# Twelve rows of inverse sums turned and spread by DMA in a two-layer graph attention kernel, with new slots

## The reference, cut to what matters

```
h = relu(layernorm(x))                       # before each layer
# layer 0: q, k, v = h W + b; scores = q k^T / sqrt(32) + beta * adj, masked where adj <= 0
x = x + softmax(scores) @ v
# layer 1: q, k, v from h; a = q k^T / sqrt(384) + adj
pad_mask = all(a == 0, over the keys)        # such rows give zeros
o = nan_to_num(softmax(where(pad_mask, -inf, a))) @ v
x = x + o @ Wo.T + bo
```

## Time and profile before

| what | value |
|---|---|
| median of 3 runs | 2241.57 us |
| the profiled execution's own time | 2242.91 us |
| its span (first to last instruction) | 2241.1 us |
| PE busy | 2165.6 us, 97% |
| ACT busy | 2044.9 us, 91% |
| DVE busy | 1825.2 us, 81% |
| POOL busy | 1529.3 us, 68% |
| DMA queue of SP, share of 16 DMA engines | 69.1% |

### The profile page before, as it was taken

How to read it: one execution, slowest core, us unless ns; L and a number is a source line. 1 busy time by engine, 2 the same in 40 slices (tenths; PEclk the granted TensorE clock), 3 DMA queues, 4 the chain that set the end, 5 groups by cost and what they waited for, 6 DMA issues and landing times.

```text
span 2241.1 us, 75523 instructions
## 1 busy us (share of the span) xinstructions
PE 2165.6 (97%) x19968; PEld 1424.7 (64%) x19968; DVE 1825.2 (81%) x10186; ACT 2044.9 (91%) x7816; POOL 1529.3 (68%) x2439
## 2 busy tenths in 40 slices
PE   3889999999999999999999999999999999999997
PEld 1556666666666666666666666666666666666665
DVE  4678888888888888888888888888888888888777
ACT  3879999999999999998999999999999999999987
POOL 4458667676677676676776676776676776676565
PEclk9999999999999999999999999999999999999999
DMA  8667676886676776676776766976666887867651
GB/s 188 136 129 138 124 140 135 136 158 123 138 144 134 136 157 123 138 140 123 152 133 134 144 134 134 153 132 136 144 132 134 155 128 137 146 131 129 132 107 45
DMA packets 461311, 303.36 MB, mean 135 GB/s; under 512 B 228432, under 2 KB 460880, under 8 KB 460880
## 3 DMA queue, kind: packets, MB, share of 16 engines
q1 hardware_dynamic: 460880, 298.45, 69.1%
HBM read 71.83 MB, written 25.17 MB: 43 GB/s over the span
## 4 chain that ended last, share of the span: by engine, by line
PE 83%; DVE 6%; issue 4%; ACT 3%; POOL 1%; SPq 1%; DMA 1%; DVEq 0%; ACTq 0%; POOLq 0%
PE job_bank L886 45%; PE pt_bank L909 13%; PE o_bank L922 8%; PE score_bank L899 7%; PE inv_bank L945 3%; PE post_bank L959 2%; PE post_bank L955 2%; PE post_bank L956 2%; ACT probs L583 2%; PE post_bank L937 2%; DVE neg L691 1%; DVE part_lo L757 1%; DVE inv_wide L749 1%; DVE off_zero L740 1%; DVE live L744 1%
## 5 line engine op out<-in xcount | busy, mean ns | idle before, releaser
L583 ACT ACTIVATE probs<-neg,neg_max 128x128 f32<-128x128 f32 x3072 | 1189.6, 394 | 60.8 <-DVE neg_max L691 60.7
L886 PE MATMUL job_bank<-h,w_hi 128*128 128x512 f16 x2304 | 725.0, 381 | 41.1 <-DMA h<-h_rows 37.1
L583 ACT ACTIVATION_READ_ACCUMULATOR probs<-neg,neg_max 128x1 f32 x3072 | 595.1, 194 | 0.0
L608 ACT ACTIVATE probs_t<-pt_bank 128x512 f32<-128x512 f32 x768 | 449.8, 586 | 32.9 <-PE pt_bank L909 30.1
L909 PE MATMUL pt_bank<-ident,probs 128*128 128x128 f32 x3072 | 465.0, 274 | 10.7 <-ACT probs_t L608 9.9
L886 PE MATMUL job_bank<-h,w_lo 128*128 128x512 f16 x1152 | 438.2, 380 | 0.0
L909 PEld LDWEIGHTS pt_bank<-ident,probs 128*128 128x128 f32 x3072 | 366.7, 141 | 93.9 <-issue 13.7
L886 PE MATMUL job_bank<-w_hi,h 128*128 128x384 f16 x1536 | 414.3, 327 | 7.7 <-DVE v L771 7.5
L520 POOL TENSOR_TENSOR pair_sum<-neg 128x256 f32<-128x256 f32 x384 | 281.2, 732 | 190.4 <-DVE neg_max L691 176.1
L691 DVE CUSTOM_DVE_ANT_0 neg<-score_bank,bias 128x128 f32<-128x128 f32 x1536 | 353.9, 286 | 24.1 <-issue 22.4
L886 PEld LDWEIGHTS job_bank<-h,w_hi 128*128 128x128 f16 x2304 | 221.9, 98 | 232.7 <-issue 49.9
(11 more groups left out here) (57 smaller groups left out, 3547.0 us busy)
## 6 DMA issues: line engine op xcount, KB each, us to landing
stack<-part_hi SPq DMA_DIRECT2D x768, 128.0 KB, 3.4
stack<-part_lo SPq DMA_DIRECT2D x384, 128.0 KB, 3.6
x_norm<-in_x SPq DMA_DIRECT2D x32, 768.0 KB, 6.1
x_res<-in_x SPq DMA_DIRECT2D x32, 768.0 KB, 5.9
out_x<-result SPq DMA_DIRECT2D x128, 192.0 KB, 3.3
adj<-in_adj SPq DMA_DIRECT2D x64, 256.0 KB, 3.6
h<-h_rows SPq DMA_TRANSPOSE x256, 3.8
stack<-in_L_gnn_Wq SPq DMA_DIRECT2D x2, 576.0 KB, 7.1
```

Of the source, the lines that this page charges most:

```text
L583: last = act.activation(probs[c % 2][:, h, :], neg[c % 2][:, h, :], ACT.Exp, bias=neg_max[:, b, first + h:first + h + 1], scale=-1.0, accu ...
L608: act.activation(probs_t[b % 2][:, first:first + HC, :].rearrange("p h q -> p (h q)"), pt_bank[:, :], ACT.Copy).then_inc(probs_t_ready, 1)
L886: last = pe.matmul(to, stationary, moving, start=(m == 0), stop=(m == MATMULS - 1))
```

## The change

The multiplication into 12 x 32 copies is gone. DVE writes `inv_live`, 128 nodes by 12 heads. PE turns that alone: one transpose with 12 output partitions in place of three with 128. ACT copies 12 x 128 from PSUM to `inv_flat` (two buffers). SP then issues three DMAs per graph (`spread_inverse`): each reads 4 rows of `inv_flat` and writes each of them to 32 partitions of `inv_t` (two buffers), 128 partitions by 512 bytes. `norm_o` waits for the DMAs' semaphore.

The places move: DVE inverse (both layers) to slot 3b + 2 place 2, PE turn to slot 3b + 4 place 0, ACT copy to slot 3b + 3 place 3, the new SP step to slot 3b + 3 place 1, ahead of the transpose of h in the same slot. The product stays at slot 3b + 5 place 2. `PROJ`, `HIGH_AT`, `LOW_AT`, `NORM_SLOTS` and some places of the output steps are changed too.

```diff
-INVERSE_AT = (2, 0)
+INVERSE_AT = (0, 2)
-TURN_INV_AT = (2, 3)
-INV_T_AT = (2, 2)
+TURN_INV_AT = (2, 0)
+INV_T_AT = (1, 3)
+SPREAD_AT = (1, 1)
-NORM_SLOTS = (0, 2, 3, 5)
+NORM_SLOTS = (0, 1, 3, 6)
-HIGH_AT = ((0, 1), (0, 1), (1, 0))
-LOW_AT = ((0, 2), (0, 2), (1, 2))
+HIGH_AT = ((0, 1), (0, 1), (1, 1))
+LOW_AT = ((0, 2), (1, 0), (1, 2))
-O_LO_AT = (3, 1)
+O_LO_AT = (3, 2)
-X_MID_AT = (4, 1)
+X_MID_AT = (4, 2)
-CENTRE_AT = (1, 2)
+CENTRE_AT = (1, 3)
-STORE_AT = (9, 0)
+STORE_AT = (9, 1)
 PROJ = (
+    ((2, 0, 0), (1, 0, 2), (0, 4, 3), (7, 3, 1), (0, 0, 1), (5, 0, 2), (6, 5, 4), (0, 0, 1),
+     (8, 6, 1), (0, 1, 2), (7, 2, 2), (1, 1, 12)),
+    ((0, 5, 0), (2, 5, 0), (2, 7, 0), (6, 0, 3), (2, 5, 4), (5, 4, 3), (0, 1, 0), (7, 0, 1),
+     (3, 7, 2), (0, 0, 0), (7, 0, 0), (5, 0, 4)),
 )
+            def spread_inverse(u, b):
+                sp.wait_ge(inv_flat_ready, u.group * GROUP + (b + 1))
+                for c in range(KC):
+                    rows = inv_flat[b % 2][HC * c:HC * (c + 1), :].unsqueeze(1).to_broadcast([HC, HEAD, P])
+                    sp.dma_start(inv_t[b % 2][:, c, :], rows).then_inc(inv_t_in[b % 2], 16)
@@ copy_inverse
-                act.activation(inv_t[:, :, :].rearrange("p c q -> p (c q)"), inv_bank[:, 0:DIM],
-                               ACT.Copy).then_inc(inv_t_ready, 1)
+                act.activation(inv_flat[b % 2][:, :], inv_bank[0:HEADS, 0:P], ACT.Copy).then_inc(inv_flat_ready, 1)
@@ inverse_sums
-                dve.tensor_tensor(inv_wide[:, :, :], live[:, :].unsqueeze(2).to_broadcast([P, HEADS, HEAD]),
-                                  inv1[:, :].unsqueeze(2).to_broadcast([P, HEADS, HEAD]),
-                                  ALU.mult).then_inc(inv_wide_ready, 1)
+                dve.tensor_tensor(inv_live[:, :], live[:, :], inv1[:, :], ALU.mult).then_inc(inv_live_ready, 1)
@@ norm_o
-                dve.wait_ge(inv_t_ready, u.group * GROUP + (b + 1))
+                dve.wait_ge(inv_t_in[b % 2], (u.group * 2 + b // 2) * 48 + 48)
@@ turn_inverse
-                for c in range(KC):
-                    last = pe.transpose(inv_bank[:, P * c:P * (c + 1)],
-                                        inv_wide[:, HC * c:HC * (c + 1), :].rearrange("p h d -> p (h d)"),
-                                        ident[:, :])
-                last.then_inc(inv_turned, 1)
+                pe.transpose(inv_bank[0:HEADS, 0:P], inv_live[:, :], ident[:, :]).then_inc(inv_turned, 1)
```

More of the change, by code:

```diff
@@ L310, in build @@
         inv1 = sb("inv1", [P, HEADS])
-        inv_wide = sb("inv_wide", [P, HEADS, HEAD])
-        inv_t = sb("inv_t", [P, KC, P])
+        inv_live = sb("inv_live", [P, HEADS])
+        inv_flat = [sb(f"inv_flat{b}", [HEADS, P]) for b in range(2)]
+        inv_t = [sb(f"inv_t{b}", [P, KC, P]) for b in range(2)]
         o_t = sb("o_t", [P, KC, P])
@@ L370, in build @@
         inv1_done = sem("inv1_done")
-        inv_wide_ready = sem("inv_wide_ready")
+        inv_live_ready = sem("inv_live_ready")
         inv_turned = sem("inv_turned")
-        inv_t_ready = sem("inv_t_ready")
+        inv_flat_ready = sem("inv_flat_ready")
+        inv_t_in = [sem(f"inv_t_in{b}") for b in range(2)]
         o_turned = sem("o_turned")
@@ L444, in phase @@
                     for place in range(2):
+                        u, b = finished(p, s, place, SPREAD_AT)
+                        if of_layer(u, b, 1):
+                            spread_inverse(u, b)
                         u, b = finished(p, s, place, STORE_AT)
@@ L612, in copy_inverse @@
                 act.wait_ge(inv_turned, u.group * GROUP + (b + 1))
-                if some(u.group * GROUP + b):
-                    act.wait_ge(o_norm_ready, u.group * GROUP + b)
-                act.activation(inv_t[:, :, :].rearrange("p c q -> p (c q)"), inv_bank[:, 0:DIM],
-                               ACT.Copy).then_inc(inv_t_ready, 1)
+                if some(u.group * GROUP + (b - 1)):
+                    act.wait_ge(o_norm_ready, u.group * GROUP + (b - 1))
+                act.activation(inv_flat[b % 2][:, :], inv_bank[0:HEADS, 0:P], ACT.Copy).then_inc(inv_flat_ready, 1)
             def high_o(u, b):
@@ L785, in norm_o @@
                 dve.tensor_tensor(o_norm[:, :, :].rearrange("p c q -> p (c q)"), o_bank[:, 0:DIM],
-                                  inv_t[:, :, :].rearrange("p c q -> p (c q)"), ALU.mult).then_inc(o_norm_ready, 1)
+                                  inv_t[b % 2][:, :, :].rearrange("p c q -> p (c q)"), ALU.mult).then_inc(o_norm_ready, 1)
             def make_result(u, b):
@@ L940, in turn_inverse @@
             def turn_inverse(u, b):
-                pe.wait_ge(inv_wide_ready, u.group * GROUP + (b + 1))
+                pe.wait_ge(inv_live_ready, u.group * GROUP + (b + 1))
                 if some(u.group * GROUP + b):
-                    pe.wait_ge(inv_t_ready, u.group * GROUP + b)
-                for c in range(KC):
-                    last = pe.transpose(inv_bank[:, P * c:P * (c + 1)],
-                                        inv_wide[:, HC * c:HC * (c + 1), :].rearrange("p h d -> p (h d)"),
-                                        ident[:, :])
-                last.then_inc(inv_turned, 1)
+                    pe.wait_ge(inv_flat_ready, u.group * GROUP + b)
+                pe.transpose(inv_bank[0:HEADS, 0:P], inv_live[:, :], ident[:, :]).then_inc(inv_turned, 1)
             def project_out(u, b):
```

## The result

The changed kernel takes 2885.3 us (median of 4 runs, 2879.7 to 2888.3) against 2241.85 us for the kernel before beside it. The ratio is 1.2861, with a 95% interval of 1.284 to 1.2881. The forecast was 2210 us, range 2198 to 2238.

The account below looks back on a forecast made before the run. PE was taken as the bound, busy 67.13 of 67.40 us in a pair of phases. Terms -34.6 - 8.2 + 10 + 1 = -31.8 took 2242.9 to 2211.1, less 1.3 for the median: 2210 us, range 2198 to 2238.

Parts of the forecast that it names:

- PE: two transposes less: PE's turn of layer 1's inverses: one narrow transpose replaces three, saving 0.27 us a graph, 34.6 us in all.
- rival 1: PE's narrow transpose regroups the array, costing 0.32 us, not 0.11; PE gains 7.7 us, giving 2237 us; chance 0.14.
- ACT's copy: ACT's copy of the turned inverses: 0.30 us for 128 columns, against 490 ns for 384; gain 0.19 us a graph.
- SP and DMA: SP's three added DMAs: 1.5 us of issues a graph, landing 3.4 us counted zero; late h transposes lose 10 us.
- PE's wait for DVE: PE's wait for the inverses before their transposes goes, as DVE starts them earlier: 8.2 us gained.
- rival 2: Waits at DVE's new inverse place make ACT 0.3 us late four times a pair: 19 us, 2229 us; chance 0.12.
- Rival 3: Transposes of h in SP's slot 9 land too late for PE's projections: 70 us lost, 2270 us; chance 0.11.

Follow-up runs that it names:

- old_no_spread: The kernel before, at its old slots, with the narrow transpose and 12-row copy, no spread DMAs, product on a constant tile: 2202.40 us, ratio 0.9823.
- no_spread: The changed kernel without its spread DMAs; the product takes a constant tile and waits for ACT's 12-row copy: 2288.24 us, ratio 1.0206.
- unused4: The changed kernel with its three 4-row DMAs issued, but the product takes another tile and does not wait for them: 2717.69 us.
- unused16: The changed kernel with eight copies of each inverse (32 rows a DMA), the product not waiting for the DMAs: 2311.42 us.
- no_spread_late: no_spread with PE's turn of the inverses behind that of the exponentials and ACT's copy after it in the same slot: 2235.24 us, ratio 0.9963.
- copies8: The changed kernel with eight copies of each inverse before the turn, so each DMA reads 32 rows: 2418.05 us, ratio 1.0789.
- old8_room: The new way with eight copies at the old slots of the kernel before; product, output projection and result a slot later, inverses and turn moved: 2579.36 us.
- copies2: The changed kernel with two copies of each inverse before the turn, so each DMA reads 8 rows: 2462.96 us, ratio 1.0983.

## Why the prediction was wrong

The experiments split the loss, each term the difference of two runs:

| term | us | from |
|---|---|---|
| PE's saving, old slots | -39.5 | old_no_spread against before |
| new slots with it | +85.8 | no_spread against old_no_spread |
| 4-row DMAs in the queue, not waited for | +429.5 | unused4 against no_spread |
| product waits for their landing | +167.6 | after against unused4 |
| sum | +643.4 | measured +643.5 |

That it comes out is no test, since each run stands once with either sign. It is a sum along one order; in another order the terms would differ, since a wait can hide behind another.

- *PE: two transposes less.* Right. 34.6 + 8.2 = 42.8 predicted, 39.5 measured. The narrow transpose costs the 0.12 taken, and rival 1 is refuted, both for entering and for leaving. In unused4, where it follows scores, it starts 0.056 us after the last of them, which is their own distance. The form is shown as 128*12, and the rows show no drain. The Trainium skill (TensorEngine Tiling (Array Packing), Key Properties), by which a change of the tiling mode drains the TensorE, would have borne on it had the transpose been laid in a 32-column tile.
- *ACT's copy.* Predicted 0.30 us, measured 0.27 (`ACTIVATE inv_flat<-inv_bank 12x128`). DVE's busy time in old_no_spread falls by 42.5 us (1825.2 to 1782.7), where 51 were said. At the new slots it does not fall at all: 1827.8 us in no_spread, 1828.3 in the changed kernel. The last multiplication, taken at 0.22 us, lasts 0.42 us there (median; 0.17 in old_no_spread) and the step ahead of it (`live`) 0.55 (0.39). So DVE's chain was taken too short for these slots; why these steps last longer there stays open.
- *SP and DMA, "they should land as the stacked copies do, 3.4 us from issue... I count zero".* This step failed, and it carries 597 of the 643 us. The price came from rows of the stacked copies, which post 16 updates a DMA; the new DMAs read 4 rows and post 5. What I counted as 1.5 us of issues is 3.7, the transpose behind is 3.9 in place of 1.24, and the landing is 8.8 us from the first issue where 5.4 were to be had. The sum of packets gave 7 points more load on the DMA engines. The queue's share times the span rises from 1549 to 1790 us, 11 points of the old span. With 32 source rows (unused16 against no_spread) it is 4. And that sum said nothing on how the packets are shared: 384 pieces a graph on few engines.
- *PE's wait for DVE, "So the wait is gone where PE turns that chunk over 0.7 us after ACT has finished it".* This failed too, and carries 53 of the 86 us of the slots. The turn at place 0 comes 0.66 us after that of the exponentials where few projections stand between. I had written the condition (0.7 us) and DVE's chain of 1.13, and then took it as met without reading how long after ACT's end PE turns a chunk. The other 33 us lie in the rest of the new layout; rival 2 below names a likely part, and the rest stays open.
- *DVE and ACT late (rival 2).* Its sign was a wait of ACT for `neg_max` of over 100 us. In the changed kernel it is 97.5, just under, against 60.7 before. Without the DMAs the sign is there: 115.3 us in no_spread and 149.1 in no_spread_late, against 60.4 in old_no_spread. PE's wait for the turned exponentials' copy grows from 8.7 us in old_no_spread to 21.2 in no_spread_late. So the wait that rival 2 described exists at the new slots, and some of the 33 us is likely its own. It was priced at 19 us; as a cause by itself it was not tested.
- *Rival 3, transposes of h too late and the kernel slower.* The right place and the right sign, with a chance of 0.11 and a price of 70 us. Its mechanism is in unused4. Mis-sized were the issue (1.8 us against 3.7) and the hold on what stands behind. In unused4 PE's waits for h beyond the first unit's come to 207 us, where the rival's whole price was 70.

The clock may have taken a share that was not in the sum. In rows 1 it is granted at 1.00; after it is 0.91 between 900 and 1900 us. Two places of PE's timeline after show the two levels:
```profile
1656.36 0.53 PE L962 MATMUL post_bank<-w_hi,o_hi 128*128 128x384 f16 x1
1656.68 0.53 PE L963 MATMUL post_bank<-w_lo,o_hi 128*128 128x384 f16 x1
...
1662.76 0.33 PE L897 MATMUL job_bank<-w_lo,h 128*128 128x384 f16 x1
1662.92 0.33 PE L897 MATMUL job_bank<-w_hi,h 128*128 128x384 f16 x1
1666.68 0.50 PE L897 MATMUL job_bank<-w_hi,h 128*128 128x384 f16 x1 [3.42 <-DVE v L782]
1666.97 0.53 PE L897 MATMUL job_bank<-w_lo,h 128*128 128x384 f16 x1
1667.29 0.63 PE L910 MATMUL score_bank<-stack 96*128 96x128 f16 x4
```
A 384-column matmul goes by in 0.32 us at 1.2 GHz and in 0.16 at 2.4 GHz. The row at 1666.68 follows 3.4 us of standing, and the one after it goes by at the lower level again. The mean clock of 0.907 over the span puts 18.6% of it, 536 us, at the lower level. At most half of that, 268 us, could be the clock's; how much of it lay in PE's way was not measured. Between 900 and 1900 us no_spread, where PE never stands over 1.5 us, keeps 1.00 and unused4 has 0.93. The same estimate for unused4 (0.928 over its span) gives at most 194 us. With no_spread's 8 taken off, up to 186 of the 429.5 us in the table may lie in the lower clock, and up to 74 of the 167.6 (268 less 194). No run separates them.

## What to carry to other kernels

Price a new DMA from a row of the same shape, not of the same size: ask how many rows its source has, and look at how many updates it posts. With 4 source rows the last of three DMAs landed 8.8 us after the first issue, with 32 rows after 4.05, and what stood behind the 4-row ones in the queue was held. Where an engine is full, the saving on it could be read to 10% from the distance of starts, but a step that feeds it may only move to where its input's finish time, read from the trace, allows it. And the broadcast that became a DMA turned ACT's 0.5 us copy between two engines into a way of 4.05 us (copies8) or 3.4 us (old8_room) at best, and in none of the complete versions did the product, which holds a PSUM bank and its place in DVE's queue, absorb that.

## What the runs showed of the hardware that I had not expected

- A DMA of 4 source rows posts 5 semaphore updates, one of 8 rows 9, one of 32 rows 16; the last of three lands 8.8, 5.4 and 4.05 us after the first issue, with equal bytes (copies2 for 8 rows, copies8 for 32).
- In the changed kernel the third 4-row DMA in a row holds SP for 2.3 us where the first two take 0.65 and 0.60, and a DMA transpose behind three of them holds it for 3.9 us against 1.26 behind three 32-row ones (copies8). A load of the adjacency that follows them takes SP 2.1 us to issue (median) where it took 0.38.
- A transpose with 12 output columns costs PE 0.11 to 0.12 us from start to start (old_no_spread, no_spread), like one with 128.
